# A Mamba block with routed experts: the depthwise convolution goes from VectorE to TensorE

## The reference

```python
xb, z = split(rms_norm(x) @ in_proj_w)                 # 512 channels each
xc = silu(depthwise_conv(xb, conv_w, taps=4) + conv_b) # causal, per channel
dt, B, C = split(xc @ x_proj_w);  dt = softplus(dt * dt_w + dt_b)
h[t] = exp(dt * A) * h[t-1] + dt * B * xc;  y = sum_s h * C
y = ((y + xc * D) * silu(z)) @ out_proj_w + residual
x = x + layernorm(y)
```

## Time and profile before

| | us |
|---|---|
| median of 3 runs | 2994.11 |
| lowest, highest | 2989.61, 2998.72 |
| the profiled execution, its time | 2992.33 |
| its span, first to last instruction | 2990.5 |
| mean granted clock of TensorE | 0.914 |
| VectorE, TensorE busy | 2669.2, 2404.4 |

### The profile page before, as it was taken

How to read it: one execution, slowest core, us unless ns; L and a number is a source line. 1 busy time by engine, 2 the same in 40 slices (tenths; PEclk the granted TensorE clock), 3 DMA queues, 4 the chain that set the end, 5 groups by cost and what they waited for, 6 DMA issues and landing times.

```text
span 2990.5 us, 26414 instructions
## 1 busy us (share of the span) xinstructions
PE 2404.4 (80%) x8160; PEld 1144.0 (38%) x8160; DVE 2669.2 (89%) x3981; ACT 1437.6 (48%) x2288; POOL 1583.3 (53%) x1284
## 2 busy tenths in 40 slices
PE   3436797878979788887979879798887879877898
PEld 1102243433434343343434434343343434333455
DVE  2999898999999999998999999998999989899752
ACT  3454554545554454545545445554554545543321
POOL 0464564645555565655656455565655556565622
PEclk8657799998989999899999989999998989999999
DMA  2441332414223241422424142241424124142111
GB/s 83 190 141 64 101 101 90 151 47 162 81 92 118 93 148 50 162 77 73 140 84 156 51 149 68 88 148 63 154 74 149 60 96 138 59 156 71 57 50 43
DMA packets 128089, 305.13 MB, mean 102 GB/s; under 512 B 11691, under 2 KB 36556, under 8 KB 119372
## 3 DMA queue, kind: packets, MB, share of 16 engines
q1 hardware_dynamic: 127948, 303.46, 30.4%
HBM read 259.89 MB, written 43.52 MB: 101 GB/s over the span
## 4 chain that ended last, share of the span: by engine, by line
DVE 51%; PE 25%; issue 10%; ACT 7%; DMA 6%; SPq 1%; POOL 0%; DVEq 0%; ACTq 0%
DVE hs L796 18%; DVE hs L778 7%; PE Gp L399 7%; DMA dxr<-dx_d 5%; PE Up L407 5%; DVE th L937 3%; PE MY L416 3%; DVE XC L751 3%; PE Y L428 3%; DVE th L942 3%; PE FP L336 2%; DVE hs L782 2%; PE FP L362 2%; DVE hs L781 2%; ACT XB L540 1%
## 5 line engine op out<-in xcount | busy, mean ns | idle before, releaser
L681 POOL TENSOR_TENSOR hs<-hs,Cb 128x512 f32<-128x512 f32 x1024 | 1268.3, 1271 | 201.8 <-DVE hs L778 168.6
L481 ACT ACTIVATE dA<-dtr,A 128x512 f32<-128x512 f32 x1024 | 704.1, 691 | 1045.9 <-DVE hs L796 1034.6
L669 POOL TENSOR_TENSOR th<-th,cmb 128x512 f32<-128x512 f32 x256 | 324.5, 1268 | 1189.7 <-DVE hs L778 707.7
L399 PE MATMUL Gp<-x2T,Wgu 128*128 128x512 f32 x1024 | 594.8, 711 | 385.7 <-DVE th L937 385.7
L796 DVE TENSOR_TENSOR_SCAN hs<-dA,carry,hs 128x512 f32<-128x512 f32 x512 | 628.4, 1266 | 39.3 <-ACT dA L481 38.6
L796 DVE TENSOR_TENSOR_SCAN hs<-dA,hs 128x512 f32<-128x512 f32 x512 | 597.3, 1206 | 40.9 <-ACT dA L481 40.3
L407 PE MATMUL Up<-x2T,Wgu 128*128 128x512 f32 x1024 | 495.4, 606 | 0.0
L416 PE MATMUL MY<-Wdn,th 128*128 128x256 f32 x2048 | 484.9, 380 | 0.0
L416 PEld LDWEIGHTS MY<-Wdn,th 128*128 128x128 f32 x2048 | 385.9, 190 | 151.5 <-issue 109.6
L778 DVE TENSOR_TENSOR hs<-dxr,Bb 128x2048 f32<-128x2048 f32 x172 | 406.8, 2365 | 37.1 <-DMA dxr<-dx_d 16.0
L399 PEld LDWEIGHTS Gp<-x2T,Wgu 128*128 128x128 f32 x1024 | 207.1, 215 | 602.7 <-DVE th L937 357.2
(11 more groups left out here) (120 smaller groups left out, 1728.3 us busy)
## 6 DMA issues: line engine op xcount, KB each, us to landing
dxr<-dx_d SPq DMA_DIRECT2D x128, 512.0 KB, 5.9
dtr<-dt_d SPq DMA_DIRECT2D x64, 1024.0 KB, 7.6
cmb<-cm_d SPq DMA_DIRECT2D x256, 256.0 KB, 3.4
dt_d<-XB SPq DMA_DIRECT2D x16, 1024.0 KB, 5.1
dx_d<-DX SPq DMA_DIRECT2D x16, 1024.0 KB, 4.4
Bb<-bc_d SPq DMA_DIRECT2D x64, 256.0 KB, 3.2
Cb<-bc_d SPq DMA_DIRECT2D x64, 256.0 KB, 8.2
xin<-in_x SPq DMA_DIRECT2D x16, 512.0 KB, 3.6
```

The source lines that it names most:

```text
L399: mm = pe.matmul(Gp[:, :], Wgu[:, k, e, 0:DE], x2T[:, c % 2, k, :], start=k == 0, stop=k == KM - 1)
L481: act.activation(dA[h % 2][:, :], dtr[:, M % 2, beta, :], ACT.Exp, scale=A[:, k:k + 1]).then_inc(s_dA, 1)
L669: pool.tensor_tensor(th[:, q % NTH, :], th[:, q % NTH, :], cmb[:, q % 2, :], ALU.mult).then_inc(m_a, 1)
L681: pool.tensor_tensor(hv, hv, Cb[:, s, :], ALU.mult).then_inc(s_c, 1)
```

## The change

The convolution of a block becomes four matmuls with diagonal 128 x 128 weights, one for each tap, that accumulate in FP over shifted windows of XB. The diagonals (Kdiag, 16 of them) are built once by VectorE at the start. ScalarE's `f_b` now only copies; a new `f_k` evacuates the convolution with its bias into XC. F's fills get a new order: b0 in g0, k0 and b1 in g1, k1 and b2 in g4, k2 and b3 in g5, k3 in g6, and z0 to z3 go to g11 to g14, one per group. `p_xn` is cut in halves for g0 and g1, `f_silu_z` goes from g13 to g15, `e_norm` from g4 to g8. xT is a buffer of its own (it lay in DX, and waited for DX's store). The down-projection weights are no longer resident: they have four slots, and there is one load of 128 KB per expert and chunk, issued by SyncE in the expert's group; `down` waits for it.

```diff
-FILLS = ['xT0', 'xT1', 'b0', 'r0', 'b1', 'r1', 'b2', 'b3', 'z0', 'z1', 'z2', 'z3', 'x0', 'x1', 'rt', 'xp', 'ct', 'db']
+FILLS = ['xT0', 'xT1', 'b0', 'k0', 'b1', 'r0', 'r1', 'k1', 'b2', 'k2', 'b3', 'k3', 'x0', 'x1', 'rt', 'xp', 'ct', 'db', 'z0', 'z1', 'z2', 'z3']
-        Wdn = sb('Wdn', [P, NE, DM])
+        Wdn = sb('Wdn', [P, NWD, DM])
+        Kdiag = sb('Kdiag', [P, MT * TAPS, P])
-        xT = flat[:, TB * DM:].rearrange('p (q t) -> p q t', q=KM)
+        xT = sb('xT', [P, KM, CH])
...
+            def load_wd(q):
+                if q >= NWD:
+                    sp.wait_ge(m_d, q - NWD + 1)
+                sp.dma_start(Wdn[:, q % NWD, :], w_dn[:, q % NE, :]).then_inc(ld_wd[q % NWD], 16)
...
+            def f_conv(p, m):
+                c = p + 1
+                bank_free(p, f'k{m}')
+                pe.wait_ge(f_act.sem, f_act.at(c, f'raw{m}'))
+                if m == 0 and c > 0:
+                    pe.wait_ge(f_dve.sem, f_dve.at(c - 1, 'hist'))
+                for k in range(TAPS):
+                    mm = pe.matmul(FP[:, :], Kdiag[:, m * TAPS + k, :], XB[:, m, k:k + CH], start=k == 0, stop=k == TAPS - 1)
+                mm.then_inc(fp_full, 1)
...
             def down(q):
                 c, e = divmod(q, NE)
                 pe.wait_ge(m_a, q + 1)
+                pe.wait_ge(ld_wd[q % NWD], 16 * (q // NWD + 1))
...
                 if F and g in (1, 4, 5, 6):
-                    f_in(p, {1: 'b0', 4: 'b2', 5: 'z0', 6: 'z2'}[g])
+                    f_conv(p, {1: 0, 4: 1, 5: 2, 6: 3}[g])
+                if F and g >= 11 and g <= 14:
+                    f_in(p, f'z{g - 11}')
...
                 if F and g == 0:
                     f_turn(p, 1)
-                if F and g in (2, 4, 5, 6):
-                    f_in(p, {2: 'b1', 4: 'b3', 5: 'z1', 6: 'z3'}[g])
+                    f_in(p, 'b0')
+                if F and g in (1, 4, 5):
+                    f_in(p, {1: 'b1', 4: 'b2', 5: 'b3'}[g])
...
                 act.activation(XB[:, m, HIST:], FP[:, :], ACT.Copy).then_inc(f_act.sem, 1)
+
+            def f_k(p, m):
+                c = p + 1
+                act.wait_ge(fp_full, filled(p, f'k{m}'))
                 if m == 0 and c >= 2:
                     act.wait_ge(s_y, (c - 1) * GPC)
-                act.activation(XC[:, c % 2, m, :], FP[:, :], ACT.Identity, scale=conv_w[:, m, HIST:HIST + 1], bias=conv_b[:, m:m + 1]).then_inc(f_act.sem, 1)
+                act.activation(XC[:, c % 2, m, :], FP[:, :], ACT.Identity, bias=conv_b[:, m:m + 1]).then_inc(f_act.sem, 1)
...
                 if F and g == 0:
                     f_xT(p, 0)
                     f_xT(p, 1)
-                if R_ and g == 0:
-                    p_xn(p)
-                if F and g == 1:
                     f_b(p, 0)
+                if F and g in (1, 4, 5, 6):
+                    f_k(p, {1: 0, 4: 1, 5: 2, 6: 3}[g])
+                if F and g in (1, 4, 5):
+                    f_b(p, {1: 1, 4: 2, 5: 3}[g])
+                if R_ and g in (0, 1):
+                    p_xn(p, g)
...
+            for m in range(MT):
+                for k in range(TAPS):
+                    dve.tensor_scalar(Kdiag[:, m * TAPS + k, :], ident, conv_w[:, m, k:k + 1], None, ALU.mult)
...
-                if F and g in (2, 3, 5, 6):
-                    conv(p, {2: 0, 3: 1, 5: 2, 6: 3}[g])
+                if F and g == 7:
+                    keep_history(p)
```

More of the change, by code:

```diff
@@ L162, in sandwich_kernel @@
         e_act = Steps(sem('e_act'), ['xr'])
-        f_act = Steps(sem('f_act'), ['xT0', 'xT1', 'raw0', 'tap0', 'raw1', 'tap1', 'raw2', 'tap2', 'raw3', 'tap3', 'z0', 'z1', 'z2', 'z3', 'silu_x', 'xd', 'dt', 'silu_z'])
-        f_dve = Steps(sem('f_dve'), [f'c{k}{m}' for m in range(MT) for k in range(HIST)] + ['hist', 'dx'])
+        f_act = Steps(sem('f_act'), ['xT0', 'xT1', 'raw0', 'k0', 'raw1', 'k1', 'raw2', 'k2', 'raw3', 'k3', 'silu_x', 'xd', 'dt', 'z0', 'z1', 'z2', 'z3', 'silu_z'])
+        f_dve = Steps(sem('f_dve'), ['hist', 'dx'])
         fp_full = sem('fp_full')
@@ L180, in sandwich_kernel @@
         ld_cm = [sem(f'ld_cm{k}') for k in range(2)]
+        ld_wd = [sem(f'ld_wd{k}') for k in range(NWD)]
         st_dt, st_dx, st_xd, st_cm = (sem(k) for k in ('st_dt', 'st_dx', 'st_xd', 'st_cm'))
@@ L184, in sandwich_kernel @@
         early = [(Cst, consts), (Cols, cols), (Win, w_in), (A, alog), (Wx, w_x), (SelDt, sel_dt)]
-        late = [(Wout, w_out), (Wrt, w_rt), (Ebias, ebias), (Wgu, w_gu), (Wdn, w_dn)]
+        late = [(Wout, w_out), (Wrt, w_rt), (Ebias, ebias), (Wgu, w_gu)]
         def filled(p, f):
@@ L254, in _ @@
                     load_cm(q)
+                q = expert_at(G)
+                if q is not None:
+                    load_wd(q)
                 if in_f(p):
@@ L415, in down @@
                 for b in range(TB):
-                    mm = pe.matmul(MY[b // 2][:, (b % 2) * DM:(b % 2 + 1) * DM], th[:, q % NTH, b * P:(b + 1) * P], Wdn[:, e, :], start=e == 0 and b % 2 == 0, stop=e == NE - 1 and b % 2 == 1)
+                    mm = pe.matmul(MY[b // 2][:, (b % 2) * DM:(b % 2 + 1) * DM], th[:, q % NTH, b * P:(b + 1) * P], Wdn[:, q % NWD, :], start=e == 0 and b % 2 == 0, stop=e == NE - 1 and b % 2 == 1)
                 mm.then_inc(m_d, 1)
@@ L546, in keep_ends, with p_xn @@
                 act.activation(carry[:, k:k + NBETA], hs[:, G % NH, :, CH - 1], ACT.Copy).then_inc(s_keep, 1)
-            def p_xn(p):
+            def p_xn(p, k):
                 c = p - 1
[L550 to L553, removed]
+                if k == 0:
+                    act.wait_ge(ld_x[c % 2], 16 * (c // 2 + 1))
+                    act.wait_ge(e_dve.sem, e_dve.at(c, 'nbr'))
+                    act.wait_ge(st_dx, 16 * min(p + 1, NC))
+                for b in (2 * k, 2 * k + 1):
                     ins = act.activation(rn[:, b, :], x1[:, c % 2, b, :], ACT.Identity, scale=ln1[:, c, 0, b:b + 1], bias=ln1[:, c, 1, b:b + 1])
@@ L622, in _ @@
                     f_xT(p, 1)
-                if R_ and g == 0:
-                    p_xn(p)
-                if F and g == 1:
                     f_b(p, 0)
+                if F and g in (1, 4, 5, 6):
[4 more added lines that the diff above has]
+                    p_xn(p, g)
                 if R_ and g in (2, 3):
                     p_rev(p, g - 2)
[L629 to L633, removed]
                 if R_ and g == 4:
                     p_ro(p)
-                if F and g in (5, 6):
-                    f_z(p, 2 * g - 10)
-                    f_z(p, 2 * g - 9)
+                if F and g >= 11 and g <= 14:
+                    f_z(p, g - 11)
                 if R_ and g == 6:
@@ L657, in _ @@
                     z_norm(p - 2)
-                if F and g == 13:
+                if F and g == 15:
                     f_silu_z(p)
-                if 0 <= p + 2 < NC and g == 4:
+                if 0 <= p + 2 < NC and g == 8:
                     e_norm(p + 2)
@@ L740, in ep_newton, with keep_history @@
                 newton(n_dve, k, 'r', ep_w[:, :, c0:c1])
-            def conv(p, m):
+            def keep_history(p):
                 c = p + 1
[L744 to L757, removed]
+                dve.wait_ge(fp_full, filled(p, f'k{MT - 1}'))
+                if c % HALVES < HALVES - 1:
+                    dve.tensor_scalar(XB[:, :, 0:HIST], XB[:, :, CH:CH + HIST], 1.0, None, ALU.mult).then_inc(f_dve.sem, 1)
+                else:
+                    dve.memset(XB[:, :, 0:HIST], 0.0).then_inc(f_dve.sem, 1)
             def f_dx(p):
```

12 lines of the change are left out of this document (5 added, 7 removed).

## The result

| | kernel before | changed kernel |
|---|---|---|
| median of 18 runs each | 2995.78 us (2989.61 to 3000.63) | 3002.93 us (3000.99 to 3009.4) |
| ratio, 95% interval | | 1.0026 [1.0018, 1.0033] |
| span of the profiled execution | 2990.5 us | 2999.5 us |

A forecast was written before the change was run, and what follows sets the result against it. TensorE, full in g1 to g3, was taken to make VectorE wait. Even chunks -2.1, odd -4.5, loads +6, start +7.3, first two chunks -12: 2992.3 - 5.3 + 1.8 = 2988.8, said 2989 us; range 2976 to 3003, 2950 to 3022 with B and C.

The forecast's parts named there:

- the stretch g0 to g7: Chunk 8, gate of g0 to gate of g7: DVE loses 9.3 us and waits 9 us more; distance stays 78.5 us.
- It and `down` behind it take some 1.8 each: TensorE from g0: `b0` and `down` take some 1.8 us each, so `gate` of g1 starts 2.8 us later.
- the hole: TensorE in g0: `b0` stands behind the second transpose and xT1's evacuation, so cannot start before 1443.7.
- the first two chunks' term: First two scanning chunks: convolution's 9.3 us really go, a cold `b0` costs about 4 us; 12 us gained for the two.
- The odd chunks' -0.6: Odd chunks, which scan with a carry and are longer on DVE: 0.6 us gained in each of six.
- The loads' term: Streamed weight loads delay the dxr loads in g15: 0.4 us in each of 15 chunks, 6 us lost.
- 2.4 for `f_silu_z`: `f_silu_z` moved to g15, with two table loads: 0.4 us charged in each of six odd chunks, bounds 0 to 1.28.
- The start: Kernel start: four blocks alternate fill and convolution in one bank, delaying the silu; 7.3 us lost.
- A: Rival: VectorE stays the bound, so its removed convolution time and most of the idle come off; 2840 us, chance 0.05.
- The rule weighed against the trace beforehand: Judge TensorE's headroom by weight-load busy time: 38% against VectorE's 89%, so VectorE is the engine to relieve.
- B: Rival: PE's order gives more room, DVE waits 6.5 instead of 9 us in 13 full chunks; 2956 us, chance 0.22.
- C: Rival: late convolution evacuations in g1, g4, g5 make PE wait, 2 us per chunk slower; 3015 us, chance 0.28.

The follow-up runs named there:

- experiment 4: Changed kernel with one convolution tap instead of four in block 0 alone: 2968.81 us, ratio 0.9908 against the kernel before.
- experiment 5: Changed kernel with one convolution tap instead of four in blocks 1, 2 and 3: 2995.47 us, ratio 0.9996 against the kernel before.
- experiment 7: Changed kernel with convolution blocks 0 and 1 back on VectorE, b0 and b1 back in g1 and g2: 2928.07 us, ratio 0.9768 against the kernel before.
- experiment 2: Changed kernel with four zero-tile matmuls added around the second transpose of g0, nothing moved: 2993.35 us, ratio 0.9989 against the kernel before.
- experiment 3: Side by side on one chip: changed kernel with zero-tile matmuls 2995.01 us (0.9996), changed kernel again 3004.05 us (1.0019), ratios against the kernel before.
- experiment 1: Changed kernel with the down-projection of g0 moved ahead of the second transpose: 2977.8 us, ratio 0.9935 against the kernel before.
- experiment 6: Kernel before with only the streamed down-projection weights (four slots, one 128 KB load per expert): 2996.17 us, ratio 0.9995.

## Why the prediction came out on the wrong side

**The part that held** is the mechanism: TensorE is full in g1 to g3, the convolution's 9.3 us come back as waits, and the stretch g0 to g7 stays. Chunk 8, whose g1 to g6 are 0.3 us shorter than before, can be compared instant by instant in the first execution, when 1437.97 - 1434.71 = 3.26 us are added to the forecast's times: `gate` of g1 1450.61 forecast, 1450.65 measured; `expert_up` of g4 after `up` of g3 1482.70, 1482.82; `gate` of g4 on TensorE 1484.43, and it stands at 1484.35; VectorE's gate of g7 1516.56, 1516.54. A block's convolution on TensorE is 1456.99 - 1453.45 = 3.54 us from start to start (3.55 forecast), read from the timeline:

```profile
1453.45 3.70 PE L355 MATMUL FP<-XB,Kdiag 128*128 128x512 f32 x8
1456.99 1.88 PE L426 MATMUL Up<-x2T,Wgu 128*128 128x512 f32 x4
```

DVE's busy time is 2533.6 (2523 forecast) and 84%, PE's 2572 (2600). Experiments 4, 5 and 7 show the path itself by changing it. That chunk 8 fits so well is in part luck: in the second execution its `b0` is slow and the same times are past.

**The step that failed** is "It and `down` behind it take some 1.8 each", in the stretch g0 to g7. The step is right for `down` and, in 5 chunks of 13, for `b0`. In the other 8 `b0` is 1 to 1.8 us longer (2.94 to 3.75 us in place of 1.95), since it was put behind a hole that the same step had worked out ("`b0` can't start before 1443.7, whatever PE does"): I priced the hole as lateness and not as what it does to the clock of the first work behind it. The half clock stood as the upper bound for the convolution, one instruction too late, and the cold fill of 3.55 us was in the earlier trace rows, the cold `b0` itself in the first two chunks' term. The full chunks' g1 to g6 came to +10.7 and not -5.7 us; of the 16.4 us between, 10.9 (experiment 2) to 11.9 (experiment 3) are the clock. The Trainium skill (TensorE: Matmul & The Clock Gate, HAM oscillation) tells of bursts of matmuls that start at the lower clock after each wait for data, and advises to order the loop so that TensorE stays busy. The trace agrees in 8 of 13 chunks, with 3.65 against 1.96 us in chunk 9, and experiment 1 is that advice.

**The rest of these 16.4 us,** some 5, is that the chunks with a quick `b0` come to about 0 and not to -0.3 or -0.6 each: with zero matmuls the 13 chunks sum to -0.2 and +0.4. The odd chunks' -0.6 had been "worked in the same way", with no timeline of theirs shown. No run tells what these 5 us are.

**The loads' term, +6,** was wrong in place and size. Experiment 6 puts it at 0.9995 [0.9986, 1.0004], and g15 with g0 is +0.1 in the changed kernel, +2.0 the second time. The later data are there in the waits (5.3 us in experiment 6), half of them in g11, which the prediction had only in its upper bound, and in experiment 6 the waits for Y went down by as much. The +6 that did not come in g15, and 2.4 for `f_silu_z` beside it, hid a part of the 16.4 that did: 2989 was too near because of them, by luck.

**Smaller terms.** The start: first inputs at 88.32, 8.0 us later than before (7.3 forecast). Four blocks take 7.2 us each there, from the timeline of the start, beside the earlier trace rows:

```profile
12.29 3.22 DVE L724 TENSOR_SCALAR Kdiag<-Cst,Cols 128x128 f32<-128x128 f32 x16
...
26.29 3.75 PE L345 MATMUL FP<-xT,Win 128*128 128x512 f32 x4 [0.78 <-ACT xT L521]
...
35.27 1.98 PE L345 MATMUL FP<-xT,Win 128*128 128x512 f32 x4 [0.78 <-ACT XC L536]
...
42.48 1.98 PE L345 MATMUL FP<-xT,Win 128*128 128x512 f32 x4 [0.78 <-ACT XC L536]
...
49.69 1.98 PE L345 MATMUL FP<-xT,Win 128*128 128x512 f32 x4 [0.78 <-ACT XC L536]
```

The first two chunks gained 10.6 (12 forecast). The cold gate of g7 went, as said: g7 and g8 gain 4.9 (0.55 x 6 = 3.3 forecast). `f_silu_z` in g15, charged with 2.4, shows in +0.1 for g15 and g0. g9 to g14, taken as 0, came to +6.4 and, the second time, +3.0. Of it g11 has +4.3 and +4.0, and in experiment 6, which moves no fill, it has +4.4: so this seems to go with the loads and not with the z fills (all 11 profiles with streamed weights have +1.1 to +4.6 there, against a single one of the kernel before). g10, with +2.4 and -0.6, is scatter.

**The rivals.** A (2840) is denied: VectorE's work went and the time stayed. The rule weighed against the trace beforehand (the Trainium skill, Perfetto Trace Analysis, Identifying the Most-Contended Engine) pointed there. TensorE's weight loads are at 41% now, and it still is the engine that VectorE waits for; what decides is that it is full in the 35 us of the chunk, from `b0` to the `up` of g3, where its lateness is passed on. B, that a part comes back, did not happen in the changed kernel, for there is no room on TensorE in g1 to g3; experiment 1 makes 1.7 us of room per chunk and gets it. C has the right sign but another cause: its price was gaps in g1, g4 and g5 that end with ScalarE's XC. The fills' wait for XC is 18.8 us over the whole kernel, in 9 places, and all of them lie at the start (three of 0.78) and in the first two chunks; in the 13 full chunks there is none, and TensorE has no gap at all from the end of `b0` to the `gate` of g7.

## What to carry to other kernels

Work moved to an engine that has slack on average pays only in the groups where that engine has it: cut the period into its groups first, and split the work between the engines if need be (two blocks each gave 0.9768, all four 1.0026, and 0.9935 in a better order). Before a matmul is put behind a wait on a path without slack, price it at both clocks, and look whether something independent can go into the hole; here `down`, moved ahead of a transpose and a fill, gave 25 us of 3003. A cause that costs 1 to 1.8 us in some chunks and nothing in others is found by the length of each group over all chunks, not by one chunk: the one that the forecast was worked out on was one of the five where the cause is absent, and in a second execution it was present there.

## What the hardware showed that I had not expected

- Two holes, of 1.69 to 2.28 and of 0.78 us, with 0.66 us of matmuls between them, are followed by a `b0` at the lower clock in 8 and 9 of 13 chunks in two executions of the same kernel, and only 4 of these chunks are the same. In chunk 8 of the first the fall comes some instructions earlier.
- 2.1 us of zero matmuls per chunk (1.46 + 0.60 in experiment 2) cost nothing measurable and keep `b0` at 1.95 or 1.96 us in all 26 full chunks of two profiles.
- 256 more loads of 128 KB (2.1 MB in each chunk) left g15, where the DMA share was 0.91 already, within some tenths of a us on average as long as it was; g11 is 0.1 to 0.35 us longer in each chunk than before, in all 11 profiles with these loads.
- Taking 71 us of work from TensorE (experiment 5) put its `gate` of g7 back to the lower clock, 3.78 instead of 1.98 us in chunk 9, and g7 and g8 became 6.4 us longer.
